# Gated memory stage: VectorE's normed and gated outputs in other places of its turn, and twelve of sixteen indirect scatters a turn earlier

## What is computed

```python
def step(carry, inp):
    M, n, m = carry
    qt, kt, vt, li, lf, op = inp
    m_next = jnp.maximum(lf + m, li)
    i_s = jnp.exp(li - m_next)
    f_s = jnp.exp(lf + m - m_next)
    M = f_s[:, :, None] * M + i_s[:, :, None] * (vt[:, :, None] * kt[:, None, :])
    n = f_s * n + i_s * kt
    h_raw = jnp.einsum('bij,bj->bi', M, qt)
    denom = jnp.maximum(jnp.abs(jnp.einsum('bi,bi->b', n, qt))[:, None], 1e-06)
    h = jax.nn.sigmoid(op) * (h_raw / denom)
    return ((M, n, m_next), h)
...
idx = jnp.argmax(probs, axis=-1)
...
buf = jnp.zeros((E, C, D), dtype=h.dtype).at[idx, pos_safe].set(x, mode='drop')
```

## Time and profile before

| | us |
|---|---|
| runs before, median (lowest to highest of 3) | 3205.5 (3203.17 to 3209.28) |
| profiled execution, its own time | 3203.23 |
| its span, first to last instruction | 3201.0 |
| TensorE busy | 2796.7 (87%) |
| VectorE busy | 2419.8 (76%) |
| ScalarE busy | 2174.9 (68%) |
| GpSimd busy | 1914.1 (60%) |
| the 400 scatters (L689), busy, and idle before them | 469.3, 115.4 |

### The profile page before, as it was taken

The page is one execution under the profiler, slowest core; times in us unless marked ns, Lnnn a source line. Parts: engine busy times, 40 slices in busy tenths (PEclk is TensorE's granted clock), DMA queues, the critical chain, the costliest instruction groups (busy, mean ns, idle before and its releaser), DMA issues. The chain is left out here.

```text
span 3201.0 us, 68718 instructions
## 1 busy us (share of the span) xinstructions
PE 2796.7 (87%) x25818; PEld 1558.3 (49%) x25818; DVE 2419.8 (76%) x3224; ACT 2174.9 (68%) x3138; POOL 1914.1 (60%) x1191
## 2 busy tenths in 40 slices
PE   7999999969999999995499958799989898989897
PEld 5666666635555555553244413344444444444444
DVE  6888888858888888884387638787878787878783
ACT  6777777758888878872144437676777777777672
POOL 8888888811677777777200066666666665656531
PEclk9999999989999999996799959999999999999999
DMA  1111111111221222211444421112212121212111
GB/s 48 42 42 39 41 41 42 40 59 36 62 72 55 73 56 56 62 42 51 141 151 152 140 57 36 37 46 54 58 47 62 44 62 49 56 49 56 47 36 51
DMA packets 208269, 191.21 MB, mean 60 GB/s; under 512 B 76381, under 2 KB 163398, under 8 KB 207562
## 3 DMA queue, kind: packets, MB, share of 16 engines
q1 hardware_dynamic: 173850, 142.95, 15.4%
q0 software_dynamic: 25600, 26.01, 3.6%
q10 hardware_dynamic: 8496, 17.87, 1.5%
HBM read 99.08 MB, written 87.65 MB: 58 GB/s over the span
## 5 line engine op out<-in xcount | busy, mean ns | idle before, releaser
L2418 POOL DMA_INDIRECT E_row<-yb,P_gi x400 | 401.1, 1003 | 395.5 <-POOLq L93 302.0
L2425 POOL TENSOR_TENSOR E_w<-E_w,E_rs 128x1024 f32<-128x1024 f32 x200 | 393.8, 1969 | 406.4 <-DVE E_rs L2333 406.4
L689 POOL DMA_INDIRECT xb<-B_yt,P_gi x400 | 469.3, 1173 | 115.4 <-issue 113.8
L204 POOL TENSOR_TENSOR A_kmask<-A_ksb,A_pack_a 128x3584 f32<-128x3584 f32 x56 | 356.3, 6363 | 115.2 <-ACT A_ksb L374 115.2
L2218 ACT ACTIVATE E_w<-E_w 128x1024 f32<-128x1024 f32 x200 | 211.8, 1059 | 252.8 <-DVE E_w L2326 252.0
L2330 DVE TENSOR_REDUCE E_sm<-E_w 128x16 f32<-128x1024 f32 x200 | 243.9, 1220 | 138.7 <-ACT E_w L2218 136.9
L2318 DVE TENSOR_REDUCE E_mx<-E_lg 128x16 f32<-128x1024 f32 x200 | 237.6, 1188 | 63.0 <-PE E_lg L1983 62.9
L474 DVE COPY A_vbd<-A_v 128x512 f32<-128x512 f32 x336 | 215.6, 684 | 74.1 <-PE A_v L324 74.1
L2326 DVE TENSOR_TENSOR E_w<-E_lg,E_mx 128x1024 f32<-128x1024 f32 x200 | 244.1, 1220 | 4.6
L2014 PEld LDWEIGHTS E_wt<-S_pack_f,E_w 128*128 128x128 f32 (+1 forms) x1600 | 174.7, 141 | 139.5 <-issue 105.2
L1983 PE MATMUL E_lg<-S_wxs,E_yo 64*128 64x512 f32 x800 | 229.2, 649 | 9.7 <-DVE E_w L2326 9.6
(11 more groups left out here) (321 smaller groups left out, 6830.9 us busy)
## 6 DMA issues: line engine op xcount, KB each, us to landing
R_xs<-xb SPq DMA_DIRECT2D x57, 256.0 KB, 2.7
yb<-R_ys SPq DMA_DIRECT2D x57, 256.0 KB, 2.0
B_x<-h SPq DMA_DIRECT2D x25, 512.0 KB, 4.3
h<-B_hh SPq DMA_DIRECT2D x25, 512.0 KB, 3.2
A_xg<-in_xw SPq DMA_DIRECT2D x56, 224.0 KB, 2.5
h<-A_res ACTq DMA_DIRECT2D x56, 224.0 KB, 2.6
E_hx<-h SPq DMA_DIRECT2D x48, 256.0 KB, 2.9
out<-E_ob SPq DMA_DIRECT2D x96, 128.0 KB
```

Of the source, the lines that this page charges most:

```text
L204: nc.gpsimd.tensor_tensor(kmask[i % 2][:], bc(ksb[i % 2][:].unsqueeze(2), [128, J, H, Q]), bc(head_of_row[:].unsqueeze(1).unsqueeze(3), [1 ...
L689: pool.indirect_dma_start(out=xb, out_offset=bass.IndirectOffsetOnAxis(ap=routed.gi[0:k, c, b:b + 1], axis=0), in_=yt[c % LT][0:k, D * row ...
L2418: pool.indirect_dma_start(out=row[b % LR][:, k, i], out_offset=None, in_=yb, in_offset=bass.IndirectOffsetOnAxis(ap=idx[:, c, 2 * n + i:2 ...
L2425: TT(w3, w3, bc(rs[g % 3][:].unsqueeze(2), [128, 2 * SH, G]), ALU.mult).then_inc(w_done, 1)
```

## The change

VectorE's list gets another order and GpSimd's scatters another split. No instruction is added or taken away on any engine, and TensorE's, ScalarE's and SyncE's lists stay.

```diff
@@ GpSimd
                 for t in range(CHUNKS + 5):
                     at(weigh_keys, t - 1)
-                    at(scatter, t - 5, range(0, 5))
+                    at(scatter, t - 5, range(12, B))
                     at(age_memory, t - 2)
                     at(scale_memory, t - 1)
-                    at(scatter, t - 5, range(5, B))
+                    at(scatter, t - 4, range(0, 12))
@@ VectorE
                 for t in range(CHUNKS + 4):
-                    at(outputs, t - 2)
                     at(ends, t - 1)
...
                     at(own, t - 4)
+                    at(slots, t - 4)
+                    at(numbers, t - 4)
                     at(norm_sum, t - 1)
-                    at(slots, t - 4)
                     at(gate_out, t - 1)
-                    at(numbers, t - 4)
                     at(norm_weight, t - 1)
+                    at(norm_query, t - 1)
+                    at(normed_out, t - 2)
                     at(forget_middle, t)
-                    at(norm_query, t - 1)
+                    at(outputs, t - 1)
                     at(forget_sum, t)
                     at(last_max, t - 1)
                     at(last_norm, t - 1)
-                    at(normed_out, t - 2)
```

## The result

| | before | after |
|---|---|---|
| runs, median (lowest to highest of 4 each), us | 3207.39 (3203.17 to 3215.81) | 3251.62 (3249.55 to 3253.83) |
| ratio, 95% interval | | 1.0139 (1.0126 to 1.0153) |
| span, us; mean granted clock | 3201.0; 0.962 | 3247.5; 0.953 |

A forecast was written before the change was run, and what follows sets the result against it. TensorE's wait for VectorE's yy was taken to bound the gated memory stage, GpSimd next with about 1.6 us a turn to spare. Terms -5, +42 and -15 sum to +22: 3228 us, range 3178 to 3252.

The forecast's parts named there:

- the two-beat case: Gated memory stage: late and early turns alternate, a pair 65.0 us; kernel 3207 to 3250, forecast 3228, chance 0.56.
- VectorE's part: Gated memory stage: yy ready before attend ends, TensorE's wait gone, turn of TensorE and VectorE 28.2 us instead of 30.6.
- the walk: GpSimd's queue stepped along VectorE's with port waits: L669 alternately late and early, mean 32.5 us a turn.
- The two rules of the walk: Scatter starting under a two-SBUF-input VectorE instruction ends 0.8 us after it; of GpSimd multiply and such instruction, later waits.
- Rival 4: Scatters wait for no port; GpSimd free at 2.8 in every turn, turn 28.5 us, -66, 3140 us; chance 0.03.
- the late turn's length: Turn 5 and its like: scaled memory comes late, so the turn lasts 35.8 to 36.9 us instead of 28.2.
- rival 3: TensorE's clock falls behind pauses in the ten late turns, up to 8.8 us each: 3240 to 3320 us; chance 0.06.
- the start: The two turns before the first scatter (t of 2 and 3): 2 x 2.4 = 5 us saved.
- the tail: GpSimd alone behind the last L669: twelve scatters fewer (68 for 80) at 1.28 us each, -15 us.
- Rival 1: Steady even turns of 29.6 us in the gated memory stage, -42 us: 3163 to 3196; chance 0.25.
- Rival 2: No net change: milder late turns of 33 to 34, about 31.5 us a turn, 3199 to 3211; chance 0.10.

The follow-up runs named there:

- half of the scatters: The changed kernel with eight scatters of each chunk in the turns, the other eight behind the last turn, values wrong; 3364.9 us, turns 28.1 to 28.4.
- eight for twelve: The change with GpSimd issuing four older scatters, the memory pair, four more older, then eight (not twelve) of the newer chunk; 3211.47 us, ratio 1.0010.
- gate_out moved: gate_out moved from behind slots to behind normed_out, against the kernel before with seven scatters of each chunk a turn sooner; 3208.24 us, ratio 1.0005.

## Why the prediction was wrong in size

The time, 3251.6, lies just inside the stated range and just outside the two-beat case's own 3207 to 3250; the change costs 44 us where 22.5 was forecast.

**Right: VectorE's part.** TensorE's wait for yy is gone but for 0.45 in some early turns, and the turn without GpSimd is 28.15 (half of the scatters) for 28.2.

**Right: the walk.** Late and early turns alternate from t = 5; L669 at 8.9 (8.9), hh ready at 12.3 (12.4), numbers at 18.2 (17.0), mems at 21.3 (21.1 to 22.2), the early L669 at 0.6 to 1.8 (2.5), the early turn 28.2 to 28.8 (28.6 to 29.0). The two rules of the walk held: the scatter under the scan took 2.66 to 2.90, and of a GpSimd multiply and a VectorE instruction with two SBUF inputs the later one waited (hh 3.09). Where the two start within half a us, the rows do not tell which will wait; two such cases stand in the last section. One kind was missing: the copy of the numbers to int32 (L1298, one input), 0.17 in the early turn, took 1.29 beside L682. Rival 4 fell, since scatters wait beside scans in every kernel here. The note of the Trainium skill that would have it so (SBUF — State Buffer, section "SBUF: two separate sides") names only a VectorE instruction in a two-port mode, such as an fp32 copy, as holding up DMAs that GpSimd issues; the trace does not agree, with 2.66 to 2.90 under scans.

**Wrong: the late turn's length, +15 in the sum.** "So this turn lasts 28.2 + 7.6 to 8.7 = 35.8 to 36.9" counts only how late mems is. It measured a mean of 38.0, and the pair 66.5 for 65.0. What failed is that the prediction put the clock apart as rival 3, with 0.06, at up to 8.8 us a turn, and left it at zero in its own case. It does fall in each late turn, for the first two groups only: turn_memory takes 1.97 in all ten of them and variance_out 3.6 to 3.8 or, in every second one, 2.6 to 2.9, which is 2.5 or 1.6 us in all. With TensorE kept at work (the repeated matmuls) the turns are 35.9 and 29.6, a pair of 65.5, half a us from the forecast. So 1 of the 1.5 us a pair is the clock. The trace of before had a sign of it that the prediction did not read: a `denominator` of 3.45 behind a pause of 2.39, in a turn of 32.1 (and one of 3.41 in another, of 32.0), while the clock of the whole stretch rounds to 1.00:

```profile
1089.77 3.45 PE L711 MATMUL B_PD<-B_nq,B_pack_b 128*128 128x512 f32 x4 [2.39 <-DVE B_yy L1213]
```

**Wrong: the start, +5.5.** "2 x 2.4 = 5 us saved" was nothing: L669 of turn 4 starts at 790.41 for 789.89. The turns before the first scatter are not the steady ones on which 2.4 was read; they lasted 26.9 and 29.7 in before, and 26.8 and 28.1 here, and L669 stands at 0.6 of its turn for 0.2. That is 1.2 us saved. Ahead of them the first `rms` comes 1.7 later (734.88 for 733.16). Of this 0.95 is there at the first y already; y stands at 695.4 to 697.3 in the twelve traces, so this part is not clearly the change's. From there to the first `rms` it is 38.4 us here, 37.8 to 38.0 in the five other kernels with VectorE's new order, and 37.5 to 37.7 in five of the six with the old one: so 0.2 to 0.4 us are the order's, and the rest differs from trace to trace.

**Wrong: the tail, +3.4.** 15 forecast, 11.6 measured. Twelve scatters fewer are 15.4, but behind the last turns GpSimd waits for the numbers again:

```profile
1529.63 1.01 POOL L689 DMA_INDIRECT xb<-B_yt,P_gi  x1 [2.73 <-DVE P_gi L1298]
1532.14 0.97 POOL L689 DMA_INDIRECT xb<-B_yt,P_gi  x1 [1.50 <-issue]
```

**The sum.** Measured: +0.5, +57.3 in the turns, -11.6, which is +46.2; forecast -5, +42, -15, which is +22. All three terms erred in one direction.

**The rivals.** Rival 1 (a steady turn of 29.6, faster) did not occur in any kernel. Even turns did, with VectorE's order alone and with eight for twelve, but at 30.8 and 31.3, since the port waits are 5.5 a turn and not 4.1. That was its weak term, and it made the 0.25 too high. Its condition, few tenths that decide who gets the port, is borne out with gate_out moved, where half a us at L669 makes the turn 0.8 longer. Rival 2 fell, since its late turns were to be 33 to 34. Rival 3 came half true: its condition held in every late turn, but it cost 1.6 to 2.5 us and not 8.8, since the clock is back before `project_o`.

## What to carry to other kernels

A wait that one engine sheds is a gain only up to the next engine's turn: add to GpSimd's work the waits that the new order brings, phase by phase, before the new turn is taken from TensorE's and VectorE's lists alone. On a queue that issues in order, put the work that another engine waits for ahead of filler, and filler where the queue would wait. Where a step makes TensorE pause for some us, count the clock behind the pause into that step, and not into a case apart.

## What the runs showed of the hardware that was not expected

- Behind a pause of 5.79 us the clock was 0.53 for 5.6 us, and turn_memory was as slow in all the late turns. Shorter pauses went either way: behind 2.4 us `denominator` took 1.96 in most turns of before and 3.45 and 3.41 in two; behind 2.6 (scatters alone) 1.96, 2.74 and 3.53 in turn; behind 1.99 (gate_out moved) 1.96 in most turns and 2.4 to 3.7 in five. So the length of the last pause does not decide alone; what does was not settled.
- A VectorE scan and a GpSimd multiply that start close together run one behind the other, and the order of their rows does not tell which waits. The scan at 956.16 waits for the multiply at 956.61 and ends 2.18 behind it (5.01 for 2.30); the multiply at 902.47 waits for the scan at 902.29 and ends 0.85 behind it (2.96 for 1.04).
- VectorE's copy with a change of type (16 numbers) took 1.29 for 0.17 beside a GpSimd multiply (901.08 and 901.27).
